# Macaron block with retention: second FFN of six chunks moved to the end, first FFN of two chunks moved behind the first projections

## What is computed

```python
x = x + 0.5 * ffn(layernorm(x), weight, bias)
x = x + attn(layernorm(x), Wq, Wk, Wv, W_G, W_O)
x = x + 0.5 * ffn(layernorm(x), weight, bias)

# ffn: blocks of 32 elements of a row, of x and of the weight
scales = max(max(abs(blocks)) / 7.5, eps); q = nearest value of the fp6 e2m3 grid
out = (xq * xs) @ (wq * ws).T + bias

# attn: 8 heads of 128, gamma_h = 1 - 2**(-5-h)
scores = (q @ k.T) / sqrt(128) * gamma**(n-m)   # for n >= m, else 0
ret = (scores @ v), normalized per head (mean, variance)
out = (silu(X @ W_G) * ret) @ W_O
```

## Time and profile before

| | |
|---|---|
| median of 3 runs | 553.67 us |
| profiled execution, its own time | 553.52 us |
| span of its slowest core (core 2), first to last instruction | 551.5 us |
| spans of the 8 cores | 546.0 to 551.5 us |
| mean granted TensorE clock of the cores | 0.960 to 0.972 |
| busy: PE, VectorE (DVE), ScalarE (ACT), GpSimd (POOL) | 445.1, 359.1, 192.0, 259.0 us |
| moved by DMA | 54.20 MB, mean 98 GB/s |

### The profile page before, as it was taken

One profiled execution on the slowest core, in us unless ns is written; L12 is line 12 of the kernel. 1 busy time (PEld: TensorE's weight loads), 2 busy tenths in 40 slices (PEclk: granted clock), 3 DMA queues, 4 the chain that ended last, 5 costly groups with the idle time before them and its releaser, 6 DMA issues.

```text
span 551.5 us, 8259 instructions; the slowest of 8 cores (546.0 to 551.5 us)
## 1 busy us (share of the span) xinstructions
PE 445.1 (81%) x2417; PEld 220.0 (40%) x2464; DVE 359.1 (65%) x656; ACT 192.0 (35%) x271; POOL 259.0 (47%) x328
## 2 busy tenths in 40 slices
PE   0212746986899999999999999998999999998544
PEld 0111313442445454545454545454544444454212
DVE  2888873553568696969696868565556556465450
ACT  0444313435060606151524342414425243340310
POOL 0665888614165555555555454423332452424322
PEclk9999987999899999999999999999999999999686
DMA  7999996371314354565446444433344332413000
GB/s 225 290 198 198 211 160 105 55 119 30 66 35 82 110 83 118 78 126 86 116 91 106 96 59 102 76 64 76 58 77 100 91 74 62 77 54 62 39 38 38
DMA packets 98395, 54.20 MB, mean 98 GB/s; under 512 B 87728, under 2 KB 87984, under 8 KB 98352
## 3 DMA queue, kind: packets, MB, share of 16 engines
q1 hardware_dynamic: 91488, 37.93, 32.0%
q0 software_dynamic: 5280, 10.49, 13.1%
q10 hardware_dynamic: 1584, 5.28, 2.8%
HBM read 34.28 MB, written 8.39 MB: 77 GB/s over the span
## 4 chain that ended last, share of the span: by engine, by line
PE 44%; DVE 25%; issue 13%; ACT 7%; POOL 6%; DMA 2%; DVEq 1%; ACTq 0%; POOLq 0%; SPq 0%
PE p L628 40%; DVE arena L331 5%; DVE arena L341 3%; ACT arena L526 3%; DVE arena L344 3%; DVE arena L413 2%; POOL arena L847 2%; DVE arena L394 2%; DVE arena L346 2%; DVE arena L316 2%; DMA arena<-wf 1%; ACT arena L558 1%; ACT arena L505 1%; PE pstate L750 1%; DVE arena L404 1%
## 5 line engine op out<-in xcount | busy, mean ns | idle before, releaser
L628 PE MATMUL p<-arena 128*128 128x512 bf16 x1745 | 402.6, 387 | 36.3 <-ACT arena L558 19.9
L628 PEld LDWEIGHTS p<-arena 128*128 128x128 bf16 x1792 | 175.8, 99 | 248.4 <-issue 55.4
L331 DVE BATCH_NORM_STATS2 arena<-arena 128x6 f32<-128x512 f32 x96 | 66.4, 691 | 8.9 <-DVE arena L377 3.1
L526 ACT ACTIVATE arena<-p,arena 128x128 bf16<-128x128 f32 x128 | 46.4, 467 | 65.5 <-POOL arena L848 65.5
L750 PE MATMUL pstate<-arena 128*128 128x128 bf16 x176 | 17.3, 262 | 59.5 <-POOL arena L811 46.3
L514 ACT ACTIVATE arena<-arena 128x1024 bf16<-128x1024 f32 x16 | 19.9, 1241 | 117.2 <-POOL arena L835 117.2
L877 POOL TENSOR_TENSOR arena<-arena 128x1024 bf16<-128x1024 fp8e4 x16 | 30.5, 1909 | 63.0 <-DVE arena L346 63.0
L815 POOL TENSOR_SCALAR arena<-arena 128x1 f32<-128x1 f32 x48 | 11.0, 228 | 81.5 <-DVE arena L333 80.2
L868 POOL TENSOR_TENSOR arena<-arena 128x1024 bf16<-128x1024 fp8e4 x16 | 30.7, 1916 | 38.2 <-DVE arena L346 36.1
L341 DVE TENSOR_REDUCE arena<-arena 128x32 f32<-128x1024 f32 x32 | 38.9, 1215 | 11.6 <-ACT arena L498 5.9
L346 DVE SCALAR_TENSOR_TENSOR arena<-arena 128x1024 fp8e4<-128x1024 f32 x32 | 42.2, 1317 | 3.7 <-DVE arena L345 0.5
(11 more groups left out here) (46 smaller groups left out, 406.8 us busy)
## 6 DMA issues: line engine op xcount, KB each, us to landing
out<-arena SPq DMA_DIRECT2D x16, 512.0 KB, 2.7
arena<-x ACTq DMA_DIRECT2D x10, 512.0 KB, 9.7
arena<-wf SPq DMA_DIRECT2D x8, 512.0 KB, 11.3
arena<-x SPq DMA_DIRECT2D x6, 512.0 KB, 3.9
arena<-wk POOLq DMA_DIRECT2D x2, 1024.0 KB, 21.3
arena<-wq POOLq DMA_DIRECT2D x2, 1024.0 KB, 21.5
arena<-wv POOLq DMA_DIRECT2D x2, 1024.0 KB, 19.0
arena<-wg POOLq DMA_DIRECT2D x2, 1024.0 KB, 17.5
```

The source lines that it names most:

```text
L331: step(e.bn_stats(bn_ln[:, n, 6 * half:6 * half + 6], x[:, 512 * half:512 * half + 512]))
L526: e.activation(z_sb[:, h * 128:(h + 1) * 128], P1[:, h * 128:(h + 1) * 128], AF.Identity, scale=gn_a[:, h:h + 1], bias=gn_nb[:, h:h + 1]). ...
L628: last = e.matmul(pair[:, half * 512:half * 512 + 512], lhs[:, kc, :], w[:, kc, half * 512:half * 512 + 512], start=(kc == 0), stop=(kc == ...
```

## The change

- f1 of chunks 0 to 2 only comes ahead of the projections of chunk 0 (before: 0 to 4, and 5 as the first of step 0). f1(3) and f1(4) stand in step 1, from step 2 on step i does f1(i+3). Its quantization is done in step i for chunk i+5 (3 and 4 in step 0, 5 and 6 in step 1).
- f2 of chunks 0 to 8 stay in the loop (steps 3 to 11). f2 of 9 to 15 come behind it, between the last products. Their transposed inputs lie in buffers that are free by then (`late_home`).
- Projections in the order K, Q, G, V. Which pair a product takes is planned by `psum_users`, and `emptied` waits for the evacuation of the product that had the pair last. In steps 3 to 11 K and G take P2, Q takes P0 and V takes P1.
- Two k buffers. On ScalarE `evK` stands ahead of `xc2`; `evG(i)` closes step i. In steps 13 to 15 (from LATE on) K stands ahead of the scores on PE, and `evK` ahead of `norm` on ScalarE.
- The casts of wk are issued ahead of everything else on GpSimd, then wq, wg, wv with tiles 0 to 5 of wf, wo behind xd1(2). The ring of x has 10 places; ScalarE loads chunks 1 to 4, SyncE 5 to 7 once f1(0) and K(0) are done.
- Only z of chunk 15 and the last f2's input are still turned by PE at the end.

```diff
+FIRST = 3
+F2_IN = 9
+LATE = 13
+        if i < 3 or i == LATE - 1:
+            order += [("f1", f1_in(i)[0], 0), ("sc", i - 1, 1)]
+            order += [("f1", f1_in(i)[1], 2) if i == 1 else ("wo", i - 2, 2)]
+            order += [("ret", i - 1, 1), ("k", i, 0), ("q", i, 2), ("g", i, 0),
+                      ("v", i, 2)]
+        elif i < LATE:
+            order += [("f1", f1_in(i)[0], 0), ("sc", i - 1, 1), ("f2", i - 3, 2),
+                      ("ret", i - 1, 1), ("wo", i - 2, 0), ("k", i, 2), ("q", i, 0),
+                      ("g", i, 2), ("v", i, 1)]
+        else:
+            a, b = (0, 2) if i % 2 == 1 else (2, 0)
+            order += [("k", i, a), ("sc", i - 1, 1), ("wo", i - 2, b), ("ret", i - 1, 1),
+                      ("q", i, a), ("g", i, b), ("v", i, a)]
+    order += [("sc", 15, 1), ("f2", 9, 2), ("ret", 15, 1), ("wo", 14, 0), ("f2", 10, 2),
+              ("f2", 11, 0), ("wo", 15, 1), ("f2", 12, 2), ("f2", 13, 0), ("f2", 14, 2),
+              ("f2", 15, 1)]
...
+        def emptied(kind, c):
+            pair, before = USERS[(kind, c)]
+            if before:
+                nm, per = EMPTIED[before[0]]
+                e.wait_ge(sem[nm], per * (before[1] + 1))
+            return pairs[pair]
...
         def evK(c):
             e.wait_ge(sem["t_k"], c + 1)
-            if c >= 1:
-                e.wait_ge(sem["t_upd"], c)
...
-            e.copy(k_sb, P2[:]).then_inc(sem["s_evK"], 1)
+            if c >= 2:
+                e.wait_ge(sem["t_upd"], c - 1)
+            e.copy(k_sb[c % 2], pair_of("k", c)[:]).then_inc(sem["s_evK"], 1)
...
+        for i in range(1, NC):
+            if i < LATE:
+                if i + 1 < NC:
+                    tn(i + 1)
+                scopy(i - 1)
+                for c in q1_in(i):
+                    xc1(c)
                 norm(i - 1)
+                evK(i)
+                if i >= 2:
+                    xc2(i - 2)
+                evQ(i)
...
         mask(NC - 1)
+        ev2(9)
         gn(NC - 1)
-        ev2(NC - 3)
         evO(NC - 2)
+        ev2(10)
         zmul(NC - 1)
         q2(NC - 2)
+        ev2(11)
         evO(NC - 1)
```

More of the change, by code:

```diff
@@ L74, with f1_in, q1_in, psum_users @@
 Z_PE = NC - 1
[L75 to L79, removed]
+X2_PE = NC - 1
+TURNS = (["w%d" % j for j in range(KC)] + ["x0", "x1", "x2", "t0", "t1", "x3", "k0",
+                                           "q0", "x4"]
+         + ["z%d" % Z_PE, "y%d" % X2_PE])
 TURN_NO = {nm: i for i, nm in enumerate(TURNS)}
+def f1_in(i):
+    if i == 1:
+        return [3, 4]
+    return [i + 3] if 2 <= i and i + 3 < NC else []
+def q1_in(i):
+    if i == 0:
+        return [3, 4]
+    if i == 1:
+        return [5, 6]
+    return [i + 5] if i + 5 < NC else []
+def psum_users():
+    order = [("f1", 0, 0), ("f1", 1, 1), ("f1", 2, 2),
+             ("k", 0, 0), ("q", 0, 1), ("g", 0, 2), ("v", 0, 1)]
+    for i in range(1, NC):
[15 more added lines that the diff above has]
+              ("f2", 15, 1)]
+    users, last = {}, {}
+    for kind, c, pair in order:
+        users[(kind, c)] = (pair, last.get(pair))
+        last[pair] = (kind, c)
+    return users
+USERS = psum_users()
+EMPTIED = dict(f1=("v_ev1", 1), sc=("v_mask", 1), ret=("s_norm", H), f2=("v_ev2", 1),
+               wo=("v_evO", 1), k=("s_evK", 1), q=("s_evQ", 1), v=("v_evV", 1),
+               g=("s_evG", 1))
 def build_program():
@@ L133, in build_program @@
     x_sb = [f32at(o, D) for o in x_off]
-    xc1_sb = [f32at(take(4096), D) for _ in range(2)]
+    o_xc1 = [take(4096) for _ in range(2)]
+    xc1_sb = [f32at(o, D) for o in o_xc1]
     xc2_sb = f32at(take(4096), D)
@@ L148, in build_program @@
     o_qt = take(2048)
-    k_sb = bfat(o_k, D)
+    k_sb = [bfat(o_k, D), bfat(take(2048), D)]
     q_sb = bfat(o_q, D)
@@ L428, in prog_vector @@
                 st1(0)
-            if j == 3:
-                st1(1)
             if j == 5:
                 q1(0)
[L433 to L449, removed]
+            if j == 6:
+                st1(1)
+        st1(2)
+        q1(1)
+        q1(2)
+        ev1(0)
+        st2(0)
+        ev1(1)
+        st1(3)
+        st2(1)
+        q1(3)
+        ev1(2)
+        st1(4)
+        q1(4)
+        evV(0)
+        for i in range(1, NC):
+            for c in f1_in(i)[:1]:
+                ev1(c)
+            mask(i - 1)
+            for c in f1_in(i)[1:]:
+                ev1(c)
             if i + 1 < NC:
                 st2(i + 1)
-            if 0 <= i - 3:
+            if i == 2 or i >= LATE - 1:
+                evO(i - 2)
+            if 3 <= i < F2_IN + 3:
                 ev2(i - 3)
[L454 to L458, removed]
+            for c in q1_in(i):
+                st1(c)
+            gn(i - 1)
+            if 3 <= i < LATE - 1:
                 evO(i - 2)
-            if 0 <= i - 1:
+            if i < LATE:
                 zmul(i - 1)
-            if 0 <= i - 2:
+            if i >= 2:
                 q2(i - 2)
+            if i >= LATE:
+                zmul(i - 1)
             evV(i)
-            if i + AHEAD + 2 < NC:
-                q1(i + AHEAD + 2)
+            for c in q1_in(i):
+                q1(c)
         mask(NC - 1)
+        ev2(9)
         gn(NC - 1)
-        ev2(NC - 3)
         evO(NC - 2)
+        ev2(10)
         zmul(NC - 1)
         q2(NC - 2)
+        ev2(11)
         evO(NC - 1)
-        ev2(NC - 2)
+        ev2(12)
         q2(NC - 1)
-        ev2(NC - 1)
+        ev2(13)
+        ev2(14)
+        ev2(15)
     def prog_scalar(e):
@@ L788, in prog_tensor @@
         wo(NC - 1)
-        for c in (NC - 2, NC - 1):
-            e.wait_ge(sem["g_xd2"], c + 1)
-            turn("y%d" % c, xd2_sb)
-            f2(c)
+        f2(12)
+        f2(13)
+        f2(14)
+        e.wait_ge(sem["g_xd2"], NC)
+        turn("y%d" % X2_PE, xd2_sb)
+        f2(NC - 1)
     def prog_gpsimd(e):
@@ L911, in prog_gpsimd @@
+        b1(0)
+        sm1(2)
+        xd1(1)
+        b1(1)
+        xd1(2)
+        e.wait_ge(sem["v_wy"], KC)
+        cast_load("wo", 0)
+        cast_load("wo", 1)
+        sm2(0)
+        b1(2)
+        sm1(3)
+        sm2(1)
+        xd1(3)
+        b1(3)
+        sm1(4)
+        b1(4)
+        xd1(4)
+        for i in range(1, NC):
             if i + 1 < NC:
                 sm2(i + 1)
-            if i + AHEAD + 2 < NC:
-                sm1(i + AHEAD + 2)
-            if 0 <= i - 1 < NC:
-                smG(i - 1)
@@ L926, in build_program @@
+        smG(NC - 1)
+        sm3(NC - 2)
+        xd2(NC - 2)
+        b2(NC - 2)
+        sm3(NC - 1)
+        xd2(NC - 1)
+        b2(NC - 1)
     with nc.Block() as block:
```

319 lines of the change are left out of this document (157 added, 162 removed).

## The result

| | before | after |
|---|---|---|
| median | 553.65 us (4 runs) | **584.41 us** (4 runs) |
| ratio, 95% interval | | **1.057** [1.054, 1.061] |
| span of the slowest core | 551.5 us | 582.5 us (core 7) |
| spans of the 8 cores | 546.0 to 551.5 us | 579.3 to 582.5 us |
| mean granted TensorE clock of the cores | 0.960 to 0.972 | 0.942 to 0.949 |

The forecast was 565.5 us with a range of 549 to 578. The direction was right, the time lies 18.9 us above the forecast and outside the range.

The account below looks back on a forecast made before the run. PE and a ring from mask through norm and evV back were taken as nearly balanced. V(15) at 518.1 plus tail 40.7 gave 558.8, with clock 4.8 563.6, then +2.0 and 0.15: 565.5 us, range 549 to 578.

Parts of the forecast that it names:

- the clock term of steps 3 to 10: Time lost to half clock behind PE's idle gaps in steps 3 to 10: 4.8 us, bounds 0 and 13.6.
- The start: Up to K of chunk 0: K(0) at 79.0, 1.5 us wf delay included; 22.2 us sooner, net gain 11.8.
- No wait, with 4 us to spare: Chunk 0's V: its weight wv is there at 87, and V wants it at 90.8.
- the sum of engine time, 84 us from 3 on: DMA time of four weights, eight wf tiles, eight chunks and bias: 58 + 26 = 84, so wv at 87.
- Steps 1 and 2: G(1), f1(5) and G(2) start after 9, 10 and 7 us idle, each adding 1.7 half clock; V(2) ends 171.4.
- Steps 3 to 10: G waits for evK in each step: 28.85 us a step, PE idle 2.85; eight take 230.8, without clock loss.
- The ring: Loop's cycle from mask through statistics, group norm, norm, xc2, q2, evV, q1, ev1 to mask; nearly balanced with PE.
- with 6 in 16, 0.6 x 8 = 4.8: Steps 3 to 10: half-clock loss at the rate of the earlier kernel's gaps, six of sixteen slowed: 4.8 us.
- The upper bound: Steps 3 to 10: half clock behind the gap in every step, 8 x 1.7 = 13.6 us.
- Steps 11 to 15: Step 11 26.7, step 12 27.8 + 1.7, step 13 19.1, steps 14 and 15 20.3 each; V(15) ends at 518.1.
- The tail: After V(15): nine products, score, return, turns, waits and the end make 40.7 us against 49.5 before, gain 8.8.
- D: wf gets half the DMA engines or wv lands after 90.8; up to 6.4 us more, 568 to 580; chance 0.12.

Follow-up runs that it names:

- e7: The changed kernel with ScalarE's scaling of the bias moved behind the last weight tile of wf and xc1(1); ratio 1.056 [1.053, 1.060].
- e2: The changed kernel with nine matmuls of zeros between Q and G in steps 3 to 11; 575.17 us, ratio 1.040.
- e4: The kernel before with only the projection order changed to K, Q, G, V from step 1 on; 595.81 us, ratio 1.077.

## Why the prediction was too low

The path and the waits were forecast rightly; terms were priced too low. The step that failed most is the clock term of steps 3 to 10, set at 4.8 and measured at 11.8. The spells and waits of the other steps were priced too low as well.

**The start: nearly right, in part by luck.** K(0) at 79.0 was forecast, 79.38 measured. But not for the reason given: the first tile of wf was on VectorE at 9.45 us, as before (9.50), so the casts of wk took nothing from it. What was lost went to the wait for the bias, as e7 shows: f1(0) began at 61.29 against 56.97 before, and in e7, where the scaling of the bias stands later, at 56.50. Some 3 of these 4.3 us came back, since the third f1 ran at the full clock (3.61 where before had 5.30) and a wait of 1.05 ahead of its turn fell away. That a delay of 1.4 was left, where 1.5 had been set, is luck.

"No wait, with 4 us to spare" for wv was wrong: V(0) waited 1.55 and started at 92.79, forecast 90.8. The step that failed is the sum of engine time, 84 us from 3 on. The DMA engines did work without a pause up to wv's landing at 92.5 (a mean busy share of 1.00 from 0 to 92.5), but they moved 198 GB/s x 92.5 us = 18.3 MB, while the transfers in the sum come to 17.3 MB (an estimate: four weights of 2.10 MB, and 17 pieces of 0.52 MB). That GpSimd's queue issued the last cast only at 50.36 matters little (e7).

The Trainium skill ("DMA: Bandwidth & Descriptors", Queues, rings and completion order) says that an engine takes turns between its queues. The first wf tile shows no such loss. The cast of wk, the first in its queue, took 32.3 us to land beside wf and x, where it took 21.3 before, which agrees with it. The 45.0 of wv (the page's median in after) decides nothing: earlier casts of its own queue were ahead of it.

**Steps 1 and 2: the waits right, the spells too cheap.** Forecast idle 9, 10, 7; measured 8.78, 10.37, 7.39, each with the releaser named. Each spell was set at 1.7, from the one row behind a gap of 4.13 us. Behind 8.78 it was 2.7 (9.76 for 32 matmuls, 7.07 at full clock), behind 10.37 it was 2.9 (6.48 for 16, 3.61). Behind 7.39 it was 1.8, as set (the product run with G(2) took 12.34 for 48). With the 1.4 by which G(1) started later, and a few tenths more of idle, V(2) ends at 176.1, forecast 171.4: 4.7 too little.

**Steps 3 to 10: the mechanism right, the clock mis-sized.** A step at full clock was to be 28.85; the one on core 7 took 28.69 (289.04 to G of step 7 at 317.73). The ring was as drawn: `evK` behind `norm`, `evV` later (it begins 9.97 behind the end of `norm` in the step shown, 4.60 before; 1.69 of the difference is the spell, 3.7 the order), L423 down from 2.02 to 0.24. The term that failed is "with 6 in 16, 0.6 x 8 = 4.8": it was 7 in 8, 7 x 1.69 = 11.8. Less 0.15 a step for the shorter steps this comes near the 241.8 measured (V(10) ends at 417.9), 6.2 above the 235.6 of the forecast. The upper bound (every step, 13.6) had been written down; the fault was to take the share from before, where such gaps came now and then. That share was also miscounted: behind a third gap of before, 2.44 to 2.56 us ahead of V(2) on five cores, no spell came at all, which makes it 6 in 21. A better count of before would have led further away from the result.

**Steps 11 to 15.** 11 took 26.6, forecast 26.7. 12 took 30.8 for 29.5 (its spell was 2.9 again). 13 to 15 took 63.9 for 59.7: K(14) and K(15) waited 1.95 and 2.29 for `evG` where 1.2 each were set, and K(15) ran at the half clock (1.7). Together 5.4 too little. The products in PE's timeline that begin with G(12), K(14) and K(15):

```profile
465.50 13.45 PE L724 MATMUL p<-arena 128*128 128x512 bf16 x48 [5.23 <-ACT arena L623]
...
496.50 3.61 PE L724 MATMUL p<-arena 128*128 128x512 bf16 x16 [1.95 <-ACT arena L637]
...
518.47 5.30 PE L724 MATMUL p<-arena 128*128 128x512 bf16 x16 [2.29 <-ACT arena L637]
```

**The tail** took 43.3, forecast 40.7. The five waits on core 7 add up to 4.4 where 3 were set, and `ev2`, the store and the end 4.6 where 4.3 were; the rest, 0.9, is scattered. It is 6.2 shorter than before, not 8.8.

The sum of these, 4.7 + 6.2 + 5.4 + 2.6, is 18.9, the whole difference. (The last line of the prediction's sum has a slip: 563.6 + 2.0 + 0.15 is 565.75, not 565.5.) Some 12 of it are clock: 7.0 in steps 3 to 10, and 5.1 more than set with G(1), f1(5), G(12) and K(15) (1.0, 1.2, 1.2, 1.7). No rival as a whole came true. D had a right part (wv late), but V(0) started only 2.0 late. The range failed because the bounds of the clock term, of the spells in steps 1 and 2 and of the late steps were set one at a time and not added.

## What to carry to other kernels

When a product is moved, ask who empties the bank that it will write and where that evacuation stands in its engine's list: here 37 us hung on one instruction standing behind another that it doesn't need. Price a short gap on PE that recurs in every step with the half clock behind each one as a likely case, not by the share of a kernel that has few such gaps: here it came in 7 of 8. And moving an evacuation ahead pays only until it waits for PE itself: behind that point each wait taken away is handed on.

## What the runs showed of the hardware

- PE idle for 2.08 us (once 2.37) in every step of 30.4 was followed by a granted clock of one half that cost 1.69 us in 7 of 8 steps, on all 8 cores, while gaps of 2.2 to 2.6 in before did that in 6 of 21. Zero matmuls in the gap removed it (e2). The length of the gap alone thus doesn't decide it; what does was not found.
- What a spell costs doesn't follow the gap's length either. Behind 3.13 us (e4, one core) the same 48 matmuls took 10.52, 12.21 or 13.42; in after the cost was 1.8 behind 7.39 us, 2.9 behind 5.23 and 2.9 behind 10.37. Behind the same 8.78 us, 32 matmuls took from 8.38 to 9.76 on the eight cores, where 7.07 is full clock.
- A bias transfer issued at 7.46 us landed 37.68 us later, behind eight wf tiles of its own queue and beside casts of weights from GpSimd's. A weight cast issued 12.4 us sooner landed 2.5 sooner (e7), while the DMA engines were busy throughout.
- Beside a GpSimd addition of 2.35 us VectorE's L344, otherwise 0.24 us, lasted 2.02 and ended with it; in after, where the addition ran at 234.90 and L423 at 239.73, it took 0.24. The Trainium skill ("SBUF — State Buffer", Who interferes with whom) describes the port that the two engines share as a lock held for a whole instruction, and these rows agree.
